# Cross attention in pairs of units: scores four units ahead, output projection and next keys between transpositions and scores

## The chip, the cores and the metric

One core of one Trainium2 chip. The time is that of one execution on the device, in microseconds (us); three runs of the kernel before gave a median of 2062.98.

## What is computed

A decoder layer with post-layer-norm on x (64 sequences of 128 tokens, width 128) with a context of 120 tokens a sequence, all float32:

```
x = LN(x + linear_attention(x))        # 16 heads of width 8, cumulative sums
x = LN(x + cross_attention(ctx, x))    # 16 heads of width 64
x = LN(x + experts(x))                 # 8 experts, 2 a token, and a shared MLP
```

Cross attention, where the change is, takes x as the queries and the normalised context together with the normalised x (120 + 128 = 248 rows) as keys and values:

```
q = lat @ Wq; k, v = split(concat(LN(ctx), lat) @ Wkv)
attn = softmax(q k^T * 64**-0.5); out = (attn @ v) @ Wout
```

## The kernel before

Three stages run one behind the other, each a block with one queue of instructions per engine: linear attention, cross attention and the experts. Each engine runs its queue in the order written in the Python loops; semaphores join them. There is no planner, the order is that of the code.

`cross_attention` (line 861) works through 32 rounds `r` of two sequences. A round has 8 pairs `j` of heads; with two sequences that is 16 units `s` (unit = one sequence, one pair of heads). The stages of one unit, with the engine that has each:

- `make_G` (TensorE, line 1304): for a pair of heads, queries times the product of Wq and Wk, as a three-part float32 product (`split_product`, line 853) into the one bank `ps_G`. `G_hi` (ScalarE, line 1106) rounds it into `G_part[0]`, `G_lo` (VectorE, line 1164) subtracts to get the rest into `G_part[1]`; only then is `ps_G` free. `G_part` has two buffers.
- `scores` (TensorE, line 1315): G times the keys for two heads, 6 matmuls of 248 columns, into one of three banks of `ps_S`.
- `maxima` (VectorE, line 1178) takes minus the maximum, `exponentials` (ScalarE, line 1110) the exponentials with their sums, `inverse` (VectorE, line 1183) the reciprocal, and `weights` (GpSimd, line 1033) the product, all in one of four rings of `prob`.
- four transpositions (TensorE, line 1368) into `ps_T` (two banks), and ScalarE's copy to `probT` (line 1128).
- `weighted_values` (TensorE, line 1331), once for each gang of four units, into the one bank `ps_O`; `out_copy` (VectorE, line 1174) moves it to `outT`.

Beside this, once a round: `output` (line 1322), the projection with `wo` of the round before, into `ps_V`, and `residual` (VectorE, line 1188), which adds it to X and takes the moments; `keys` (TensorE line 1267, VectorE line 1145), which turns the next round's rows into `ps_V`; eight `make_V` (line 1311), values into the same one bank `ps_V`, each copied by `V_copy` (VectorE, line 1170). Four small jobs of the routing for the experts are spread over the round: `turn_rows`, `logits` and `ranks` on TensorE (lines 307 to 329, all in `ps_O`), `turned_rows` and `scores_of` on ScalarE, and 26 small steps on VectorE (`route`, line 331) placed by the tables `ROUTE` and `ROUTE_LATE` (line 1230). GpSimd also splits the keys into two parts (`keys_hi`, `keys_lo`), normalises rows and issues four scatters a round; SyncE loads the context and the latents of later rounds.

TensorE's `body` (line 1352) does for each unit `s`: the transpositions of unit s, then `scores` of unit s + 3 (`LEAD`). Even units follow with `make_G` of the pair three ahead, odd ones with `make_V`. The output projection stands behind `make_G` of unit 2, the next keys behind `make_G` of unit 4, and a gang's weighted values at the end of every fourth unit (0, 4, 8, 12). The turn of the rows stands ahead of unit 10's transpositions and the logits ahead of unit 11's.

VectorE's `body` (line 1201) does for each unit: the copy of V (even units), next keys (unit 5), `G_lo` (odd units), `out_copy` (units 1, 5, 9, 13), residual (unit 3), the routing steps, then `maxima` of unit s + 3 and `inverse` of unit s + 2. ScalarE's (line 1117) does exponentials of unit s + 2, the copy of the transposed unit s, and on even units `G_hi`.

The last round computes scores, G, V and keys of a round 32 that isn't used, with the inputs of the first sequences loaded again (lines 970 to 973).

Of the kernel before, what the change touches and what calls it, by code (L numbers as in the profile page):

```python
# [27 lines left out]
S = 128  # L28
# [832 lines left out]
def cross_attention(nc, X, lat, ctx, ident, tri, later, slots):  # L861
# [19 lines left out]
    LEAD = 3  # L881
# [3 lines left out]
    MADE = FIRST[1] // 2 + 2  # L885
    U32 = mybir.dt.uint32
    with ExitStack() as stack:
# [61 lines left out]
        def _(sp):  # L949
# [34 lines left out]
            for par in range(2):  # L984
                sp.wait_ge(ctx_loaded[par], (ROUNDS // 2 + 1) * 16)
                sp.wait_ge(lat_loaded[par], (ROUNDS // 2 + 1) * 32)

        @block.gpsimd
        def _(pool):
# [49 lines left out]
            def body(r, par):  # L1039
                unit = r * UNITS  # L1040
                for s in range(UNITS):
                    weights(unit + s + 2, (s + 2) % RINGS)
# [8 lines left out]
                    if s == 6:  # L1051
                        keys_hi(r + 1, 1 - par)
                    if s == 7:
                        keys_lo(r + 1, 1 - par)
# [6 lines left out]
                    if s == 11:  # L1061
                        context_deviation(r + 2)
                    if s in (12, 13):
                        normalise_context(r + 2, par, s - 12)
# [29 lines left out]
        def _(act):  # L1094
# [22 lines left out]
            def body(r, par):  # L1117
                unit = r * UNITS
                for s in range(UNITS):
                    exponentials(unit + s + 2, (s + 2) % RINGS)  # L1120
                    if s == 10 and r:
# [3 lines left out]
                    if s == 12 and r:  # L1125
                        slots.scores_of(act, r - 1)
                    act.wait_ge(T_psum, unit + s + 1)
                    nc.scalar.copy(probT[0:KT, s % (2 * GANG)], ps_T[0:KT, s % 2, :]).then_inc(probT_ready, 1)  # L1128
                    if s % 2 == 0:
                        ahead = s // 2 + 3  # L1130
                        G_hi(r * PAIRS + ahead, ahead % 2)
# [5 lines left out]
            for k in range(2):  # L1137
                exponentials(k, k)
# [3 lines left out]
        def _(dve):  # L1142
# [58 lines left out]
            def body(r, par):  # L1201
                unit = r * UNITS
                for s in range(UNITS):
                    j = s // 2
                    if s == 0 and later_round(r):
                        V_copy(r * 8 + 3, 0, 1, 1)
                    if s and s % 2 == 0:
                        k = j - 1
                        V_copy(r * 8 + 4 + k, 1 - k // 4, k % 4 // 2, k % 2)
                    if s == 5:  # L1210
                        keys(r + 1)
                    if s % 2:
                        G_lo(r * PAIRS + j + 3, (j + 3) % 2)
                    if s % GANG == 1 and (s > 1 or later_round(r)):
                        out_copy(r * GANGS + s // GANG - 1, (s // GANG - 1) % GANGS)
                    if s == 3 and later_round(r):
                        residual(r - 1)
                    if r and s in ROUTE:
                        slots.route(dve, ps_O, r - 1, *ROUTE[s])
                    if r > 1 and s in ROUTE_LATE:  # L1220
                        slots.route(dve, ps_O, r - 2, *ROUTE_LATE[s])
                    if r == MADE:
                        for k in (s,) if s < 13 else (s * 2 - 13, s * 2 - 12):
                            slots.table(dve, 0, k)
                    maxima(unit + s + LEAD, (s + LEAD) % RINGS)
                    inverse(unit + s + 2, (s + 2) % RINGS)
                    if s == 7:
                        context_moments(r + 2, par)

# [29 lines left out]
            for k in range(2):  # L1259
# [6 lines left out]
        def _(pe):  # L1266
# [85 lines left out]
            def body(r, par):  # L1352
                unit = r * UNITS
                for s in range(UNITS):
                    j, u = s // 2, s % 2

                    if s == 10 and r:
                        pe.wait_ge(outT_ready, r * GANGS + 2)
                        slots.turn_rows(pe, ps_O, ident, r - 1)
                    if s == 11 and r:  # L1360
                        slots.logits(pe, ps_O, r - 1)
                    pe.wait_ge(prob_ready, unit + s + 1)
                    if unit + s > 1:
                        pe.wait_ge(probT_ready, unit + s - 1)
                    for h in range(2):
                        for tile in range(2):
                            at = (h * 2 + tile) * S
                            last = nc.tensor.transpose(ps_T[0:KT, s % 2, at:at + S], prob[:, s % RINGS, h, tile * KT:(tile + 1) * KT],  # L1368
                                                       ident[:])
                    last.then_inc(T_psum, 1)  # L1370

                    ahead = (s + LEAD) // 2
                    if u:
                        pe.wait_ge(G_lo_ready, r * PAIRS + ahead + 1)
                    scores((unit + s + LEAD) % BANKS, (s + LEAD) % 2, par if ahead < PAIRS else 1 - par, ahead % 2)

                    if u == 0:
                        ahead = j + 3
                        pe.wait_ge(G_lo_ready, r * PAIRS + ahead)
                        if s == 10:  # L1380
                            pe.wait_ge(kT_lo_ready, r + 2)
                        make_G(ahead % 2, par if ahead < PAIRS else 1 - par, ahead % PAIRS)
                    if s == 2 and later_round(r):
                        pe.wait_ge(V_ready, r * 8 + 5)
                        output(r - 1)
                    if s == 4:
                        pe.wait_ge(V_ready, r * 8 + 4 + 2)
                        keys(r + 1, 1 - par)
                    if u:
# [553 lines left out]
```

## Time and profile before

| | us |
|---|---|
| median of 3 runs | 2062.98 (2062.4 to 2067.14) |
| the profiled execution's own time | 2065.15 |
| its span, first to last instruction | 2063.4 |
| TensorE busy | 1966.8 |
| VectorE busy | 1508.9 |
| ScalarE busy | 1278.5 |
| GpSimd busy | 1307.8 |

The stages lie at about 0 to 266 us (linear attention), 266 to 1672 (cross attention) and 1672 to 2063 (experts). TensorE's end of a matmul is modelled and lies behind the next matmul's start, so the time that a matmul takes in a queue is read from start to start. Granted clock 1.00 is 2.4 GHz, 0.50 is 1.2 GHz.

### The profile page before, as it was taken

Reading aid. Unit: us, or ns where it says so; the run is one execution under the profiler, and the core shown is the slowest. Engines: PE = TensorE matmul, PEld = TensorE weight load, DVE = VectorE, ACT = ScalarE, POOL = GpSimd, SP = SyncE. Lnnn points to the kernel's source line nnn. Section 1 sums busy time; section 2 is a strip of 40 time slices with the busy share of each in tenths; the row PEclk is TensorE's granted clock in tenths of the full one; section 3 lists DMA queues with packets and bytes.
Section 4 is the critical chain, followed back from the end, with each engine's and each line's share of the span. In section 5 each row is a group of like instructions: output and inputs, shape, how many; then the busy total and the mean of one; then the engine's idle time right before and its main releaser. Section 6 shows DMA issues by size and latency. Waiting matters only on the chain. (4 is left out here: it accounts for less than half of the span.)

```text
span 2063.4 us, 47458 instructions
## 1 busy us (share of the span) xinstructions
PE 1966.8 (95%) x16023; PEld 1704.1 (83%) x16023; DVE 1508.9 (73%) x3953; ACT 1278.5 (62%) x3908; POOL 1307.8 (63%) x1462
## 2 busy tenths in 40 slices
PE   7999879999999999999999999999999989999976
PEld 4555469999999999999999999998899878788855
DVE  5999946777777777777777777778777755455575
ACT  4777646666666666666666666666666644444455
POOL 5888746666666666666666666666666664344476
PEclk9999979999999999999999999999999989999987
DMA  4200000000000000000000000001000022222354
GB/s 133 73 18 19 18 26 1 17 17 16 16 14 22 17 16 16 17 19 17 15 16 20 16 17 17 14 21 31 20 16 16 14 62 71 84 70 70 95 158 134
DMA packets 105023, 75.78 MB, mean 37 GB/s; under 512 B 11045, under 2 KB 98677, under 8 KB 104661
## 3 DMA queue, kind: packets, MB, share of 16 engines
q1 hardware_dynamic: 93732, 53.66, 9.3%
q0 software_dynamic: 8640, 17.97, 2.6%
q8 instruction: 135, 2.21, 0.4%
q10 hardware_dynamic: 2416, 1.12, 0.2%
q14 instruction: 100, 0.81, 0.1%
HBM read 40.15 MB, written 32.57 MB: 35 GB/s over the span
## 5 line engine op out<-in xcount | busy, mean ns | idle before, releaser
L1036 POOL TENSOR_TENSOR x_prob<-x_prob,x_inv 128x496 f32<-128x496 f32 x514 | 521.6, 1015 | 460.4 <-DVE x_inv L1186 457.7
L1114 ACT ACTIVATE x_prob<-x_ps_S,x_nmax 128x248 f32<-128x248 f32 x1028 | 472.7, 467 | 226.1 <-DVE x_nmax L1180 224.4
L1180 DVE TENSOR_REDUCE x_nmax<-x_ps_S 128x2 f32<-128x496 f32 x515 | 344.8, 670 | 105.0 <-PE x_ps_S L858 97.0
L1128 ACT COPY x_probT<-x_ps_T 124x512 f32<-124x512 f32 x512 | 300.2, 586 | 166.4 <-PE x_ps_T L1368 163.8
L856 PE MATMUL x_ps_S<-x_kT_lo,x_G_hi 128*128 128x248 f32 x1030 | 328.6, 319 | 0.0
L1368 PE MATMUL x_ps_T<-ident,x_prob 128*124 128x128 f32 x2048 | 319.0, 278 | 7.7 <-POOL x_prob L1036 6.4
L1368 PEld LDWEIGHTS x_ps_T<-ident,x_prob 128*124 128x124 f32 x2048 | 233.2, 140 | 73.9 <-POOL x_prob L1036 29.9
L858 PE MATMUL x_ps_S<-x_kT_hi,x_G_hi 128*128 128x248 f32 x1030 | 285.9, 278 | 0.0
L857 PE MATMUL x_ps_S<-x_kT_hi,x_G_lo 128*128 128x248 f32 x1030 | 285.7, 277 | 0.0
L1606 POOL DMA_INDIRECT sorted_results<-e_y,w_wkv x142 | 148.8, 1048 | 169.6 <-DVE e_y L1730 160.7
L1338 PE MATMUL x_ps_O<-x_probT,x_V 124*64 124x128 f32 x4096 | 251.9, 276 | 0.4 <-ACT x_probT L1128 0.4
L1166 DVE TENSOR_TENSOR x_G_lo<-x_ps_G,x_G_hi 128x512 fp32r<-128x512 f32 x259 | 177.9, 687 | 89.5 <-ACT x_G_hi L1108 89.2
L1338 PEld LDWEIGHTS x_ps_O<-x_probT,x_V 124*64 124x64 f32 x4096 | 221.0, 137 | 18.9 <-issue 5.2
L1114 ACT ACTIVATION_READ_ACCUMULATOR x_prob<-x_ps_S,x_nmax 128x1 f32 x1028 | 206.8, 201 | 0.0
L1108 ACT CAST x_G_hi<-x_ps_G 128x512 fp32r<-128x512 f32 x259 | 152.4, 589 | 75.3 <-PE x_ps_G L858 74.7
L857 PEld LDWEIGHTS x_ps_S<-x_kT_hi,x_G_lo 128*128 128x128 f32 x1030 | 195.7, 190 | 0.0
L856 PEld LDWEIGHTS x_ps_S<-x_kT_lo,x_G_hi 128*128 128x128 f32 x1030 | 194.8, 189 | 0.0
L858 PEld LDWEIGHTS x_ps_S<-x_kT_hi,x_G_hi 128*128 128x128 f32 x1030 | 194.2, 189 | 0.0
L1172 DVE COPY x_V<-x_ps_V 124x512 f32<-124x512 f32 x259 | 175.5, 678 | 2.6 <-PE x_ps_V L858 2.6
L628 POOL TENSOR_TENSOR lin_kv<-lin_qk,lin_v 128x1024 f32<-128x1024 f32 x64 | 135.4, 2137 | 23.1 <-DVE lin_qk L740 20.2
L281 POOL DMA_INDIRECT sorted_rows<-w_rows,slots_slot x128 | 132.3, 1034 | 28.0 <-issue 23.1
L856 PE MATMUL x_ps_G<-x_kT_lo,x_M_hi 128*128 128x256 f32 x518 | 146.2, 282 | 0.1
(246 smaller groups left out, 4474.7 us busy)
## 6 DMA issues: line engine op xcount, KB each, us to landing
w_wkv<-sorted_rows SPq DMA_DIRECT2D x142, 66.0 KB
e_back<-sorted_results SPq DMA_DIRECT2D x28, 256.0 KB, 3.6
x_nk<-latents SPq DMA_DIRECT2D x34, 124.0 KB
latents<-lin_nlat SPq DMA_DIRECT2D x32, 128.0 KB, 1.8
turned_rows<-w_rows SPq DMA_DIRECT2D x32, 128.0 KB, 1.7
w_wq<-turned_rows SPq DMA_DIRECT2D x32, 128.0 KB, 2.3
out_dram<-e_result SPq DMA_DIRECT2D x16, 256.0 KB, 3.6
x_nk<-in_ctx SPq DMA_DIRECT2D x34, 120.0 KB, 2.3
```

Of the source, the lines that this page charges most:

```text
L856: nc.tensor.matmul(out, stationary[0], moving[1], start=first, stop=False)
L857: nc.tensor.matmul(out, stationary[1], moving[0], start=False, stop=False)
L858: return nc.tensor.matmul(out, stationary[0], moving[0], start=False, stop=last)
L1036: nc.gpsimd.tensor_tensor(prob[:, k], prob[:, k], inv[:, k].unsqueeze(2).broadcast_to([P, 2, K]), ALU.mult).then_inc(prob_ready, 1)
L1108: nc.scalar.copy(G_part[0][:, pair], ps_G[:]).then_inc(G_hi_ready, 1)
L1114: nc.scalar.activation(prob[:, k, h, :], ps_S[:, n % BANKS, h * K:(h + 1) * K], ACT.Exp, bias=nmax[:, k, h:h + 1], accum_out=total[:, k, h ...
L1128: nc.scalar.copy(probT[0:KT, s % (2 * GANG)], ps_T[0:KT, s % 2, :]).then_inc(probT_ready, 1)
L1166: nc.vector.tensor_tensor(G_part[1][:, pair].rearrange("p h u q -> p (h u q)"), ps_G[:], G_part[0][:, pair].bitcast(F32).rearrange("p h u ...
L1172: nc.vector.tensor_copy(V[:, hf, u, tile, :], ps_V[0:KT, :]).then_inc(V_ready, 1)
L1180: nc.vector.tensor_reduce(nmax[:, k, :], ps_S[:, n % BANKS, 0:2 * K].rearrange("p (h k) -> p h k", h=2), AX, ALU.max, negate=True).then_in ...
L1338: last = nc.tensor.matmul(ps_O[h * DH:(h + 1) * DH, k * S:(k + 1) * S], V[:, j // 4, u, tile, (j % 4 * 2 + h) * DH:(j % 4 * 2 + h + 1) * D ...
L1368: last = nc.tensor.transpose(ps_T[0:KT, s % 2, at:at + S], prob[:, s % RINGS, h, tile * KT:(tile + 1) * KT], ident[:])
```

## The change

The loops of all four engines go by pairs. On TensorE a pair is: both units' transpositions, both units' scores (of the pair two ahead, `LEAD` = 4), `make_G` of the pair three ahead, the gang's weighted values on even pairs, `make_V`. The next keys (pair 2) and the output projection (pair 1) stand between the transpositions and the scores, the turn of the rows ahead of pair 5's transpositions, the logits behind pair 5's `make_G`, the ranks behind pair 1's. The second scores of a pair wait for the exponentials of a unit three before (`exp_ready`), since four units are under way with three banks.

On ScalarE: the two copies of transposed units, the exponentials of the first unit four ahead, `G_hi`, the exponentials of the second. On VectorE: V copy, inverse of the second unit of the pair before, routing, next keys or residual, two maxima, `out_copy` on even pairs, `G_lo`, inverse, routing. The queue of GpSimd keeps its order.

In the last round everything that belonged to a round 32 is left out, and so are the two loads at the end of SyncE's queue. Ahead of the rounds a fourth unit's scores, maximum and exponentials are done.

```diff
-    LEAD = 3
+    LEAD = 4
...
@@ sync
             for par in range(2):
-                sp.wait_ge(kT_psum, ROUNDS - 1 + par)
-                load(par * 2, par)
                 slots.store_turned(sp, ROUNDS - 3 + par)
...
@@ scalar
             def body(r, par):
                 unit = r * UNITS
+                for j in range(PAIRS):
+                    if j == 5 and r:
...
+                    for s in (2 * j, 2 * j + 1):
+                        act.wait_ge(T_psum, unit + s + 1)
+                        nc.scalar.copy(probT[0:KT, s % (2 * GANG)], ps_T[0:KT, s % 2, :]).then_inc(probT_ready, 1)
+                    if j == 6 and r:
                         slots.scores_of(act, r - 1)
+                    if unit + 2 * j + LEAD < ALL:
+                        exponentials(unit + 2 * j + LEAD, 2 * j % RINGS)
+                    if r < FINAL or j + 3 < PAIRS:
+                        G_hi(r * PAIRS + j + 3, (j + 3) % 2)
+                    if unit + 2 * j + LEAD < ALL:
+                        exponentials(unit + 2 * j + 1 + LEAD, (2 * j + 1) % RINGS)
...
@@ vector
             def body(r, par):
                 unit = r * UNITS
+                for j in range(PAIRS):
+                    s = 2 * j
+                    if j == 0 and r:
                         V_copy(r * 8 + 3, 0, 1, 1)
+                    if j and (r < FINAL or j < 5):
                         k = j - 1
                         V_copy(r * 8 + 4 + k, 1 - k // 4, k % 4 // 2, k % 2)
+                    if unit + s + 3 < ALL:
+                        inverse(unit + s + 3, (s + 3) % RINGS)
+                    routing(r, s)
+                    if j == 2 and r < FINAL:
                         keys(r + 1)
+                    if j == 1 and r:
+                        residual(r - 1)
+                    if unit + s + LEAD < ALL:
+                        maxima(unit + s + LEAD, s % RINGS)
+                        maxima(unit + s + 1 + LEAD, (s + 1) % RINGS)
+                    if j % 2 == 0 and (j or r):
+                        out_copy(r * GANGS + j // 2 - 1, (j // 2 - 1) % GANGS)
+                    if r < FINAL or j + 3 < PAIRS:
                         G_lo(r * PAIRS + j + 3, (j + 3) % 2)
+                    if unit + s + LEAD < ALL:
+                        inverse(unit + s + LEAD, s % RINGS)
+                    if j == 3 and r + 1 < FINAL:
                         context_moments(r + 2, par)
+                    routing(r, s + 1)
...
             maxima(2, 2)
-            for k in range(2):
+            maxima(3, 3)
+            for k in range(3):
                 inverse(k, k)
...
@@ tensor
             def body(r, par):
                 unit = r * UNITS
+                for j in range(PAIRS):
+                    first = unit + 2 * j
+                    if j == 5 and r:
                         pe.wait_ge(outT_ready, r * GANGS + 2)
                         slots.turn_rows(pe, ps_O, ident, r - 1)
+                    for s in (2 * j, 2 * j + 1):
+                        pe.wait_ge(prob_ready, unit + s + 1)
...
+                        last.then_inc(T_psum, 1)
+                    if j == 2 and r < FINAL:
+                        pe.wait_ge(V_ready, r * 8 + 4 + 2)
+                        keys(r + 1, 1 - par)
+                    if j == 1 and r:
+                        pe.wait_ge(V_ready, r * 8 + 5)
+                        output(r - 1)
+                    ahead = j + 2
+                    if r < FINAL or ahead < PAIRS:
                         pe.wait_ge(G_lo_ready, r * PAIRS + ahead + 1)
+                        for s in (2 * j, 2 * j + 1):
+                            if s % 2:
+                                pe.wait_ge(exp_ready, (first + 3) * 2)
+                            scores((unit + s + LEAD) % BANKS, s % 2, par if ahead < PAIRS else 1 - par, ahead % 2)
+
+                    ahead = j + 3
+                    if r < FINAL or ahead < PAIRS:
+                        if j == 5:
                             pe.wait_ge(kT_lo_ready, r + 2)
                         make_G(ahead % 2, par if ahead < PAIRS else 1 - par, ahead % PAIRS)
+                    if j == 5 and r:
+                        slots.logits(pe, ps_O, r - 1)
+                    if j % 2 == 0 and first:
...
+                        gang_output(r * GANGS + j // 2 - 1)
+                    if j == 1 and r > 1:
+                        pe.wait_ge(outT_ready, r * GANGS)
+                        slots.ranks(pe, ps_O, r - 2)
+                    if r < FINAL or j < 4:
...
                             pe.wait_ge(V_ready, r * 8 + 4 + j)
...
                         make_V(par if j < 4 else 1 - par, 1 - j // 4, j % 4 // 2, j % 2)
...
             scores(2, 0, 0, 1)
+            pe.wait_ge(exp_ready, 2)
+            scores(0, 1, 0, 1)
             rounds(pe, body)
```

## Rows read from the trace of the kernel before

**Rows 1.** The page: busy us of each engine, share of the span, instructions.

```profile
PE 1966.8 (95%) x16023; PEld 1704.1 (83%) x16023; DVE 1508.9 (73%) x3953; ACT 1278.5 (62%) x3908; POOL 1307.8 (63%) x1462
```

**Rows 2.** Windows: from:to, length, each engine's busy us, then PE clock, DMA share, GB/s.

```profile
420.00:1600.00 1180.00, 1175.32 (x11107) 1081.72 (x11104) 904.37 (x2462) 782.68 (x2475) 768.19 (x907) 1.00 0.06 18
1900.00:1985.00 85.00, 77.28 (x497) 65.25 (x497) 50.95 (x165) 41.26 (x128) 45.52 (x43) 0.97 0.36 105
```

**Rows 3.** The list of waits, 420 to 1600 us: total us, times, longest.

```profile
POOL x_prob L1036 <- DVE x_inv L1186: 387.3, 300, 4.7
```

**Rows 4.** Timeline of PE, one steady round: start us, us, engine, line, operation.

```profile
938.14 3.73 PE L1327 MATMUL x_ps_V<-w_wo,x_outT 128*128 128x128 f32 x32
...
943.02 0.40 PE L856 MATMUL x_ps_V<-x_wv_lo,x_kT_hi 128*124 128x512 f32 x1
...
943.73 0.60 PE L1368 MATMUL x_ps_T<-ident,x_prob 128*124 128x128 f32 x4
944.08 0.36 PE L856 MATMUL x_ps_S<-x_kT_lo,x_G_hi 128*128 128x248 f32 x1
...
944.85 0.28 PE L856 MATMUL x_ps_G<-x_kT_lo,x_M_hi 128*128 128x256 f32 x1
...
945.57 0.59 PE L1273 MATMUL x_ps_V<-ident,x_nk 124*128 124x124 f32 x4
946.09 1.97 PE L1338 MATMUL x_ps_O<-x_probT,x_V 124*64 124x128 f32 x32
947.99 0.65 PE L1368 MATMUL x_ps_T<-ident,x_prob 128*124 128x128 f32 x4
...
958.54 0.40 PE L856 MATMUL x_ps_V<-x_wv_lo,x_kT_hi 128*124 128x512 f32 x1
...
959.43 0.41 PE L311 MATMUL x_ps_O<-ident,w_rows 128*128 128x128 f32 x2
...
980.91 0.27 PE L1327 MATMUL x_ps_V<-w_wo,x_outT 128*128 128x128 f32 x1
```

**Rows 5.** Timeline of ACT, steady stretch.

```profile
907.29 0.47 ACT L1114 ACTIVATE x_prob<-x_ps_S,x_nmax 128x248 f32<-128x248 f32 x1 [0.82 <-DVE x_nmax L1180]
...
908.20 0.58 ACT L1128 COPY x_probT<-x_ps_T 124x512 f32<-124x512 f32 x1
909.13 0.59 ACT L1108 CAST x_G_hi<-x_ps_G 128x512 fp32r<-128x512 f32 x1 [0.35 <-PE x_ps_G L858]
```

**Rows 6.** Timeline of DVE, the same round as Rows 4.

```profile
941.91 0.42 DVE L1192 TENSOR_TENSOR slots_hsum<-x_ps_V,X 128x256 f32<-128x256 f32 x1 [2.26 <-PE x_ps_V L1327]
...
943.06 0.17 DVE L389 TENSOR_TENSOR slots_place<-x_ps_O,slots_base 128x16 f32<-128x16 f32 x1
...
948.10 0.69 DVE L1176 COPY x_outT<-x_ps_O 128x512 f32<-128x512 f32 x1 [0.33 <-PE x_ps_O L1338]
...
950.66 0.59 DVE L394 TENSOR_TENSOR slots_taken<-slots_chosen,slots_place 128x32 f32<-128x32 f32 x1
...
951.58 0.67 DVE L1180 TENSOR_REDUCE x_nmax<-x_ps_S 128x2 f32<-128x496 f32 x1
...
952.51 0.69 DVE L1166 TENSOR_TENSOR x_G_lo<-x_ps_G,x_G_hi 128x512 fp32r<-128x512 f32 x1 [0.19 <-ACT x_G_hi L1108]
...
968.28 0.16 DVE L365 TENSOR_REDUCE slots_col<-slots_score 128x2 f32<-128x16 f32 x1
...
968.98 0.67 DVE L1180 TENSOR_REDUCE x_nmax<-x_ps_S 128x2 f32<-128x496 f32 x1
...
970.24 0.16 DVE L373 TENSOR_REDUCE slots_col<-slots_order 128x2 f32<-128x16 f32 x1
...
971.41 0.67 DVE L1180 TENSOR_REDUCE x_nmax<-x_ps_S 128x2 f32<-128x496 f32 x1
```

**Rows 7.** Timeline, the end of cross attention.

```profile
1665.14 0.69 DVE L1176 COPY x_outT<-x_ps_O 128x512 f32<-128x512 f32 x1 [0.71 <-PE x_ps_O L1338]
...
1665.98 3.81 PE L1327 MATMUL x_ps_V<-w_wo,x_outT 128*128 128x128 f32 x32 [0.89 <-DVE x_outT L1176]
```

More of the change, by code:

```diff
@@ L885, in cross_attention @@
     MADE = FIRST[1] // 2 + 2
+    FINAL = ROUNDS - 1
     U32 = mybir.dt.uint32
@@ L1041, in body @@
                 for s in range(UNITS):
-                    weights(unit + s + 2, (s + 2) % RINGS)
+                    if unit + s + 2 < ROUNDS * UNITS:
+                        weights(unit + s + 2, (s + 2) % RINGS)
                     if s in (1, 3) and r > 2:
@@ L1118, in body @@
                 unit = r * UNITS
-                for s in range(UNITS):
-                    exponentials(unit + s + 2, (s + 2) % RINGS)
-                    if s == 10 and r:
+                for j in range(PAIRS):
+                    if j == 5 and r:
                         if r == 1:
@@ L1136, in _ @@
                 G_hi(j, j % 2)
-            for k in range(2):
+            for k in range(4):
                 exponentials(k, k)
@@ new lines, in body, with routing @@
+                    if j % 2 == 0 and (j or r):
+                        out_copy(r * GANGS + j // 2 - 1, (j // 2 - 1) % GANGS)
+                    if r < FINAL or j + 3 < PAIRS:
+                        G_lo(r * PAIRS + j + 3, (j + 3) % 2)
+                    if unit + s + LEAD < ALL:
+                        inverse(unit + s + LEAD, s % RINGS)
+                    if j == 3 and r + 1 < FINAL:
+                        context_moments(r + 2, par)
+                    routing(r, s + 1)
+            def routing(r, s):
+                if r and s in ROUTE:
+                    slots.route(dve, ps_O, r - 1, *ROUTE[s])
+                if r > 1 and s in ROUTE_LATE:
+                    slots.route(dve, ps_O, r - 2, *ROUTE_LATE[s])
+                if r == MADE:
+                    for k in (s,) if s < 13 else (s * 2 - 13, s * 2 - 12):
+                        slots.table(dve, 0, k)
@@ new lines, in body @@
+                    for s in (2 * j, 2 * j + 1):
+                        pe.wait_ge(prob_ready, unit + s + 1)
+                        if unit + s > 1:
+                            pe.wait_ge(probT_ready, unit + s - 1)
+                        for h in range(2):
+                            for tile in range(2):
+                                at = (h * 2 + tile) * S
+                                last = nc.tensor.transpose(ps_T[0:KT, s % 2, at:at + S],
+                                                           prob[:, s % RINGS, h, tile * KT:(tile + 1) * KT], ident[:])
+                        last.then_inc(T_psum, 1)
```

89 lines of the change are left out of this document (15 added, 74 removed).

## The prediction

> **What bounds the kernel now.** I read the page first, for the shares: TensorE (PE) is busy nearly all the span [rows 1]. Then the windows by stage: in the middle of cross attention PE is busy 1175 of 1180 us at full clock, while VectorE (DVE) has 904 and ScalarE (ACT) 783 [rows 2]. The list of waits shows where the slack is: POOL spends 387 us of the stage waiting for inverses [rows 3], and DVE idles 2.26 us ahead of each round's residual, waiting for the output projection [rows 6]. PE's timeline of one round gives its length, output to output, 42.77 us (938.14 to 980.91), and the price of each group of matmuls [rows 4]. So the stage is PE's queue, end to end, 32 times. A reordering can only take out PE's small holes, or open new ones by asking for something sooner than DVE, ACT or POOL can give it.
>
> The holes are small. The values product V takes 0.71 (943.02 to 943.73), but 0.89 before the turn of the rows (958.54 to 959.43): 0.2 of waiting. The same happens once more at the round's end, so about 0.4 us a round [rows 4].
>
> **Prices on PE.** Per unit 4 transpositions to the next group 0.35, scores 0.77, the queries' product G 0.72, next keys 0.52 with the change-over behind them, a gang of weighted values (call it O) 1.90, output 3.57 (3.73 less the 0.16 below) [rows 4]. Two units of transpositions in a row: three spacings of the four make 0.60 less 0.27, so 0.11 each; TT = 0.44 + 0.35 = 0.79. The first scores record behind transpositions is 0.36 long where others are 0.28, so SS = 0.77 + 0.69 = 1.46. Together 2.25, and two separate units make 2 x 1.12 = 2.24. **Pairing itself is worth nothing.** A pair is then TT, SS, G, V = 3.67, and with O (even pairs) 5.7.
>
> O is now followed by V and not by transpositions. Four transpositions behind O last 0.65 where others last 0.60 (947.99 against 943.73): 0.05 lost. I take 0.06 for V, bounds 0 and 0.2 (the keys' change-over is 0.1). The Trainium skill (TensorE: Matmul & The Clock Gate, "Step-by-step: what each phase is for") says that PE's queue pulls weight loads ahead of running matmuls; by that the change-over would be 0 and the sum some 7 us less (4 x 0.06 x 31), but the row shows that some of it stays.
>
> **Prices on the other engines.** DVE: maximum 0.67, rest G_lo 0.69, output copy 0.69 which starts 0.11 behind O's end, V copy 0.69 as its equal in size, each freeing DVE about 0.1 before it ends; residual and moments 1.15 (941.91 to 943.06); routing steps 0.92 for the three of pair 3 (950.66 to 951.58), 0.70 for the four at the end of pair 6, 1.17 for the five of pair 7 [rows 6]. ACT: a unit's exponentials 0.91 (907.29 to 908.20), G_hi 0.59 [rows 5]. Hand-overs: PE to the others 0.2 behind the group's end (six scores records in 0.77 are 0.12 apart and 0.28 long, so the modelled end lies 0.16 past the group's, and the residual starts 0.04 behind the output's modelled end: 938.14 + 3.73 against 941.91), DVE to PE 0.15 (1665.14 + 0.69 to 1665.98) [rows 7], ACT to DVE 0.03.
>
> **What the change tightens.** (a) Scores for pair j+2 need G_lo of the G made in pair j-1. Before, three units and more lay between; now only V and TT, 1.5 us, where there is no O. The chain is G end + 0.2, G_hi 0.59, G_lo 0.69, 0.15 = 1.65 at best. G_hi also stands behind the first exponentials (0.91), which stand behind the first maximum, which stands behind whatever DVE has at the pair's head: V copy, routing, residual. (b) The output projection moves from behind G to behind TT, and still needs the V copy of the pair before (they share a PSUM bank). (c) The next keys likewise.
>
> **A round, pair by pair**, in us from PE's start of pair 1, with DVE's queue in its written order (starts are those of a steady round, where pair 0 of the next comes out as pair 0 of this one):
> - Pair 0's O ends at -0.76. DVE: output copy from -0.64, G_lo from -0.04, inverse, V copy 0.65 to 1.34. PE has TT done at 0.79, output can start at 1.49: **hole 0.70**. Output to 5.07, scores 6.46, G 7.17, the ranks' two small matmuls (0.2, an estimate from the 0.11 between two), V to 8.09.
> - Behind the output DVE has the residual 5.27 to 6.42, then the maximum to 7.09; ACT exponentials to 8.02, G_hi to 8.61; DVE G_lo to 9.33, two routing steps, V copy 9.65 to 10.34. The keys of pair 2 (due 8.88) wait for that copy till 10.49: **hole 1.61**. DVE's idle time during the 3.5 us of output no longer helps, since all of this is queued behind the residual.
> - Pair 2: scores to 12.38, O to 15.08, V to 15.84. Output copy and G_lo behind O end at 16.49, due 16.63: no hole.
> - Pair 3: DVE V copy to 17.18, three routing steps to 18.1, maximum 18.75, exponentials 19.68, G_hi 20.27, G_lo 20.99; pair 4's scores (due 20.30) start 21.14: **hole 0.84**.
> - Pair 5: the turn waits for the output copy as now: 0.20. Its G_lo (31.19) and pair 7's meet their due times with nothing left.
> - Pair 6: DVE after O: output copy, G_lo to 36.93, four routing steps to 37.62. Pair 7: V copy, five steps to 39.5, maximum 40.17, exponentials 41.1, G_hi 41.69, G_lo 42.41. Next pair 0's scores, due 40.74, start at 42.56: **hole 1.82**.
>
> Sum of holes 5.2. The round becomes 42.8 - 0.4 + 5.2 = 47.6, **+4.7**, or about 4.75 by the direct count. Thirty such intervals: +141.
>
> **What costs nothing.** A probability is due two pairs behind its scores. POOL's work is 1.74 us a unit, everything in it (768 us over 27.6 rounds of 16 units [rows 2]). Pair 3's first exponentials end at 19.68, the inverse comes behind G_lo at 21.1 and the transposition is due 26.5: covered. Tightest is the round's end, inverse at 38.3, transposition 40.2: 1.9 us for 1.74 of work. Cover gone, it would be another 1 us a round. The new wait of the second scores for the exponentials (three banks, lead four) falls due 2 us or more behind them (pair 1's at 8.02, asked for at 11.7). SP loses the two last loads and their waits; its store of turned rows and the row loads behind move up, and nobody waits for those in this trace. ACT's reordering adds no work.
>
> **Ends.** In the last round PE loses 3 units of scores (3 x 0.77), 3 G (2.2), 4 V (2.8) and the keys (0.5): 7.8, at the prices of [rows 4], of which 0.8 comes back as waits for the last probability copy: -7.0. The last round still has the holes of pairs 1 to 4, about +2. Start: the fourth scores and maximum stand ahead of the first inverse: +1. Round 0 has a few small holes of type (a): +1.
>
> **Sum.** 141 + 2 + 2 - 7 = +138 on the profiled execution's own 2065.15 (span 2063.4), which lies 0.1% above the median of 2062.98 and inside the runs shown. 2203; I say 2200. The measurement can tell about 0.3% (6 us) from no change.
>
> **Rivals.**
> 1. *The chain holds* (faster). If G_lo, V copy and output copy come in time after all, only holes go: 0.4 x 31 = -13 and -7 at the end: 2045. For it: DVE is only 77% busy, ACT 66% [rows 2]. Against: the 1.65 against 1.5 of (a) has no slack even with both engines idle. It decides where G_lo lands within 1.5 us of G. 6%; 4% for holes and gains that cancel (within 0.3%).
> 2. *Half the holes.* DVE's work is fixed, so what is late in one pair may be early in the next, and the residual's and routing's delays may be partly taken up. Only (b), the pair 0 hole and 0.3 on odd pairs: about 2 to 3 a round, 2105 to 2150. 16%.
> 3. *The clock falls too.* PE would be busy about 89% of the stage, with holes near 2 us twice a round. At 91% busy in the expert stage the granted clock was 0.97 [rows 2]. With 0.96 here, 8% of the time at 1.2 GHz, up to 4% more of 1330 us: +50, so 2250. 12%. The Trainium skill (TensorE: Matmul & The Clock Gate, "HAM oscillation — how this bites in real kernels") tells of waits between groups of matmuls that let the clock down; no row of the cross stage here shows it, as PE never pauses there.
> 4. My forecast, holes as listed with errors of a third: 2150 to 2240. 62%.
>
> The range takes 4, most of 2 and the edge of 3: 2120 to 2245. Faster 6%, same 4%, slower 90%.
>
> **What would show it.** Output-to-output near 47.5. PE idle ahead of the output (L1327's successor) and of the key transpositions, released by the V copy; ahead of scores in pairs 4 and 0, released by G_lo. In the list of waits, PE or PEld behind x_V and x_G_lo, some 100 us and more in total where there is nothing now; POOL's wait for the inverse larger. PE's busy time 8 to 10 us less. The expert stage as long as before. Wrong if the round stays under 44, or if the holes stand elsewhere, above all ahead of transpositions on POOL.

## The result and the profile after

The change makes the kernel slower: 2267.12 us (median of 4 runs, 2266.35 to 2269.51) against 2062.69 in the runs beside it, a ratio of 1.099 (95% interval 1.0968 to 1.1011). The forecast was 2200, with a range to 2245. The profiled executions differ by 201.4 us of span (2264.8 against 2063.4).

The page of the kernel after, the line that answers to [rows 1], and the stage's window that answers to the first of [rows 2]:

```profile
PE 2016.5 (89%) x15971; PEld 1731.6 (76%) x15971; DVE 1512.4 (67%) x3932; ACT 1251.3 (55%) x3897; POOL 1293.1 (57%) x1450
```

```profile
420.00:1600.00 1180.00, 1063.31 (x9612) 966.12 (x9611) 787.43 (x2123) 659.30 (x2137) 658.72 (x786) 0.98 0.05 15
```

TensorE, which had 4.7 us idle in this window, now has 117. VectorE, ScalarE and GpSimd do less in it too: nobody became the bound, all four wait for each other. So the time went into the order. The list of waits of the same window shows for whom:

```profile
POOL x_prob L1036 <- DVE x_inv L1190: 447.5, 190, 5.9
ACT x_prob L1115 <- DVE x_nmax L1184: 412.5, 190, 5.7
...
PE x_ps_S L856 <- DVE x_G_lo L1170: 79.8, 47, 2.8
...
PE x_ps_V L1288 <- DVE x_V L1176: 29.8, 24, 2.3
...
PE x_ps_V L1342 <- DVE x_V L1176: 7.0, 24, 0.4
```

The last three are the forecast's places with the forecast's releasers: scores (L856 into `ps_S`) wait for `G_lo`, keys (L1288) and output (L1342) for the V copy. 47 waits over 24 rounds are two a round. The list of before has none of them. The first answers to [rows 3].

TensorE's timeline gives the size of each hole. A pair's transpositions (8) take 0.79 from start to start where nothing waits, so what lies between their start and the next group's beyond 0.79 is the hole, the time that TensorE stands still there:

```profile
1076.30 1.18 PE L1381 MATMUL x_ps_T<-ident,x_prob 128*124 128x128 f32 x8
1080.30 0.38 PE L856 MATMUL x_ps_S<-x_kT_lo,x_G_hi 128*128 128x248 f32 x1 [2.83 <-DVE x_G_lo L1170]
...
1082.59 1.97 PE L1353 MATMUL x_ps_O<-x_probT,x_V 124*64 124x128 f32 x32
1084.49 0.49 PE L856 MATMUL x_ps_V<-x_wv_lo,x_kT_hi 128*124 128x512 f32 x1
...
1085.28 1.03 PE L1381 MATMUL x_ps_T<-ident,x_prob 128*124 128x128 f32 x8
1086.61 3.84 PE L1342 MATMUL x_ps_V<-w_wo,x_outT 128*128 128x128 f32 x32 [0.29 <-DVE x_V L1176]
1090.20 0.36 PE L856 MATMUL x_ps_S<-x_kT_lo,x_G_hi 128*128 128x248 f32 x1
...
1093.30 1.04 PE L1381 MATMUL x_ps_T<-ident,x_prob 128*124 128x128 f32 x8
1095.86 0.64 PE L1288 MATMUL x_ps_V<-ident,x_nk 124*128 124x124 f32 x4 [1.53 <-DVE x_V L1176]
```

Pair 0: 1080.30 - 1076.30 - 0.79 = 3.21. Output: 1.33 - 0.79 = 0.54. Keys: 1.77 in this round, 1.42 as the median of 22. The same reading at pair 4 gives 0.76, and the turn of rows 0.16. V behind O (1085.28 - 1084.49) takes 0.79 to 0.80 where it takes 0.70 elsewhere.

From output to output, a round was 42.8 us; now 15 of the 30 steady intervals are near 48.6, 12 near 50.15 and 3 longer (51.3, 51.4, 53.9); together 1489.3 against 1288.4, so **201 us of the 201.4 are in the rounds**. At the ends little is left over: the first output comes 5.1 later after the kernel's start, the last interval is 3.9 shorter (34.49 against 38.43), the way to the experts 1.0 longer, and the experts take 389.1 instead of 390.9.

Why 50.15? Windows (columns as in [rows 2]), two of the stretch behind one pair 0 hole, then one around the same hole a round later:

```profile
1029.50:1033.00 3.50, 2.90 (x18) 2.75 (x18) 3.33 (x11) 1.70 (x6) 1.40 (x2) 0.78 0.00 0
1033.00:1036.50 3.50, 3.50 (x36) 3.16 (x36) 1.22 (x3) 2.39 (x9) 1.63 (x2) 0.73 0.06 19
1076.00:1084.00 8.00, 5.17 (x54) 4.48 (x55) 6.65 (x18) 4.01 (x14) 3.81 (x5) 1.00 0.05 17
```

And the weighted values behind the first of these holes:

```profile
1033.07 2.84 PE L1353 MATMUL x_ps_O<-x_probT,x_V 124*64 124x128 f32 x32
```

They are 2.84 long, and 1.97 behind the second. Some matmuls of this stretch run at 1.2 GHz; it costs that round 1.55 us. Counted over the rounds: 30 x 48.6 = 1458, and 31 us lie above it, against 4 above 30 x 42.8 before. So the holes cost 30 x 5.8 = 174 us, and the 27 that are left go with the clock. They are a difference, and a few of them can be something else: two of the three longer rounds have a half-clock stretch twice as long (granted clock 0.93 over 788 to 840 and over 1334 to 1386 us), but the third, of 53.9, is the round that also makes the experts' table, which took 45.5 before.

### The profile page after: what moved, and what is told of

Read it like the earlier page. It is cut to its first block and busy times, and to the rows that moved or that the text cites. A ratio compares the mean times of both kernels' runs of the same rounds, so it can differ in the third digit from the quotient of the medians.

```text
span 2264.8 us, 47256 instructions
## 1 busy us (share of the span) xinstructions
PE 2016.5 (89%) x15971; PEld 1731.6 (76%) x15971; DVE 1512.4 (67%) x3932; ACT 1251.3 (55%) x3897; POOL 1293.1 (57%) x1450
## 3 DMA queue, kind: packets, MB, share of 16 engines
q10 hardware_dynamic: 2416, 1.12, 0.2%
## 5 line engine op out<-in xcount | busy, mean ns | idle before, releaser
L1036 POOL TENSOR_TENSOR x_prob<-x_prob,x_inv 128x496 f32<-128x496 f32 x512 | 516.7, 1012 | 672.6 <-DVE x_inv L1190 605.8
L856 PE MATMUL x_ps_S<-x_kT_lo,x_G_hi 128*128 128x248 f32 x1024 | 310.1, 303 | 102.9 <-DVE x_G_lo L1170 101.9
L1127 ACT COPY x_probT<-x_ps_T 124x512 f32<-124x512 f32 x512 | 277.6, 602 | 127.9 <-PE x_ps_T L1381 126.0
L1184 DVE TENSOR_REDUCE x_nmax<-x_ps_S 128x2 f32<-128x496 f32 x512 | 324.9, 664 | 31.8 <-PE x_ps_S L858 30.9
L856 PEld LDWEIGHTS x_ps_S<-x_kT_lo,x_G_hi 128*128 128x128 f32 x1024 | 196.4, 192 | 119.1 <-DVE x_G_lo L1170 117.8
L1381 PE MATMUL x_ps_T<-ident,x_prob 128*124 128x128 f32 x2048 | 270.4, 274 | 2.3 <-POOL x_prob L1036 2.2
L1353 PE MATMUL x_ps_O<-x_probT,x_V 124*64 124x128 f32 x4096 | 262.2, 283 | 1.1 <-ACT x_probT L1127 0.7
L1353 PEld LDWEIGHTS x_ps_O<-x_probT,x_V 124*64 124x64 f32 x4096 | 231.3, 142 | 20.0 <-issue 3.6
L1180 DVE COPY x_outT<-x_ps_O 128x512 f32<-128x512 f32 x128 | 88.5, 691 | 207.4 <-PE x_ps_O L1353 207.2
L1115 ACT ACTIVATION_READ_ACCUMULATOR x_prob<-x_ps_S,x_nmax 128x1 f32 x1024 | 212.9, 208 | 0.0
L857 PE MATMUL x_ps_G<-x_kT_hi,x_M_lo 128*128 128x256 f32 x512 | 148.9, 291 | 0.0
```

The source lines that it names most:

```text
L856: nc.tensor.matmul(out, stationary[0], moving[1], start=first, stop=False)
L857: nc.tensor.matmul(out, stationary[1], moving[0], start=False, stop=False)
L1036: nc.gpsimd.tensor_tensor(prob[:, k], prob[:, k], inv[:, k].unsqueeze(2).broadcast_to([P, 2, K]), ALU.mult).then_inc(prob_ready, 1)
L1115: nc.scalar.activation(prob[:, k, h, :], ps_S[:, n % BANKS, h * K:(h + 1) * K], ACT.Exp, bias=nmax[:, k, h:h + 1], accum_out=total[:, k, h ...
L1184: nc.vector.tensor_reduce(nmax[:, k, :], ps_S[:, n % BANKS, 0:2 * K].rearrange("p (h k) -> p h k", h=2), AX, ALU.max, negate=True).then_in ...
L1353: last = nc.tensor.matmul(ps_O[h * DH:(h + 1) * DH, k * S:(k + 1) * S], V[:, j // 4, u, tile, (j % 4 * 2 + h) * DH:(j % 4 * 2 + h + 1) * D ...
```

## Why the pair 0 hole is 3.2 us

The forecast had 1.82 there. VectorE's timeline, from the end of pair 6 through pair 7 to pair 0's wait:

```profile
1073.62 0.82 DVE L369 TENSOR_TENSOR slots_equal<-slots_score,slots_col 128x16 f32<-128x16 f32 x1
1074.48 0.17 DVE L371 SCALAR_TENSOR_TENSOR slots_order<-slots_equal,slots_index 128x16 f32<-128x16 f32 x1
1074.58 0.68 DVE L1176 COPY x_V<-x_ps_V 124x512 f32<-124x512 f32 x1
...
1075.43 1.38 DVE L375 TENSOR_TENSOR slots_chosen<-slots_order,slots_col 128x16 f32<-128x16 f32 x1
...
1077.35 1.25 DVE L1184 TENSOR_REDUCE x_nmax<-x_ps_S 128x2 f32<-128x496 f32 x2
1079.56 0.69 DVE L1170 TENSOR_TENSOR x_G_lo<-x_ps_G,x_G_hi 128x512 fp32r<-128x512 f32 x1 [0.96 <-ACT x_G_hi L1109]
```

Two steps of 16 elements take 0.82 and 1.38. In the trace before, which the forecast was priced from, they took 0.18 and 0.42. GpSimd in the same stretch:

```profile
1073.40 1.01 POOL L1036 TENSOR_TENSOR x_prob<-x_prob,x_inv 128x496 f32<-128x496 f32 x1 [2.23 <-DVE slots_col L365]
1074.59 1.12 POOL L281 DMA_INDIRECT sorted_rows<-w_rows,slots_slot  x1 [0.17 <-issue]
1075.74 1.02 POOL L1036 TENSOR_TENSOR x_prob<-x_prob,x_inv 128x496 f32<-128x496 f32 x1
```

The product ends at 74.41, the L369 step at 74.44; the next product at 76.76, the L375 step at 76.81. The small step with two SBUF inputs stands still while the product, which also reads SBUF, runs, and ends 0.03 to 0.05 us behind it. (The second step began at 75.43, ahead of that product but 0.28 before the end of GpSimd's issue of a scatter, and alone it would have been done before the product. An issue as such holds no step: the one of line 381, with two SBUF inputs too, lies wholly under the next issue and takes 0.17. What held the second step until the product began stays open.) The copy of V, which reads PSUM alone, and the maximum are not touched. The two lines over the whole kernel (least/median/most ns), before and then after:

```profile
L369 DVE TENSOR_TENSOR slots_equal<-slots_score,slots_col x32: 174/174/191, 369.3 to 1684.8; 128x16 f32<-128x16 f32 x32
L375 DVE TENSOR_TENSOR slots_chosen<-slots_order,slots_col x64: 174/176/429, 371.1 to 1687.3; 128x16 f32<-128x16 f32 x64
```

```profile
L369 DVE TENSOR_TENSOR slots_equal<-slots_score,slots_col x32: 175/824/827, 379.3 to 1888.0; 128x16 f32<-128x16 f32 x32
L375 DVE TENSOR_TENSOR slots_chosen<-slots_order,slots_col x64: 174/824/1503, 381.1 to 1890.5; 128x16 f32<-128x16 f32 x64
```

Before, the order of the queues kept the four steps of pair 6 wholly apart from the products, and the five of pair 7 met only the end of one. VectorE and GpSimd in the round that the forecast was read from:

```profile
970.43 0.42 DVE L375 TENSOR_TENSOR slots_chosen<-slots_order,slots_col 128x16 f32<-128x16 f32 x1
...
971.32 0.18 DVE L381 TENSOR_TENSOR slots_equal<-slots_rest,slots_col 128x16 f32<-128x16 f32 x1
```

```profile
969.81 1.01 POOL L1036 TENSOR_TENSOR x_prob<-x_prob,x_inv 128x496 f32<-128x496 f32 x1 [1.72 <-DVE x_inv L1186]
970.80 0.79 POOL L1012 TENSOR_SCALAR x_nk<-x_nk,x_cmom,x_crstd 120x128 f32<-120x128 f32 x1
```

The product ended at 70.82 and the L375 step at 70.85. So the standing still was there before the change, and the 0.59 of the L394 step in [rows 6] is another case of it. The change set the inverse, which starts a product, right ahead of the routing steps. Four steps at the end of pair 6 take 1.34 (forecast 0.70) and the five of pair 7 2.1 (1.17): 1.6 us more, on the chain that ends in pair 0's `G_lo`.

The Trainium skill (SBUF — State Buffer, "Who interferes with whom") says that a VectorE instruction with two SBUF inputs contends with a GpSimd instruction that reads SBUF, and that one with at most one SBUF input, outside the 2-port perf modes, doesn't. For the product the traces agree: the median of L369 is 174 ns without one beside it and 824 with one. They don't agree for every GpSimd instruction that reads SBUF: the L381 step above lies wholly under GpSimd's TENSOR_SCALAR of line 1012, which reads `x_nk` in SBUF, and takes 0.18 (174 to 176 ns in each of the 31 rounds in which it lies so).

## The experiments

The kernel before ran at 2060.71 beside the first four, and at 2063.68 beside the other four. Kernel 1 is that of experiment 1, and so on; an undisturbed round is one without half-clock stretches.

**1. Routing steps behind `G_lo`**, to get those that stood ahead of the maxima off the chain. The four at the end of pair 6 still stand ahead of pair 7's maxima.

```diff
-                    routing(r, s)
                     if j == 2 and r < FINAL:
                         keys(r + 1)
...
+                    routing(r, s)
                     routing(r, s + 1)
```

> The changed kernel, with VectorE's routing steps of a pair all behind G_lo and its inverse, none ahead of the maxima. Theory A (order of VectorE's queue: what stands ahead of the first maximum delays G_lo, and G_lo the scores two pairs later): the hole ahead of pair 0's scores shrinks from 3.2 us by the 2.0 us of the five steps to about 1.2, the one ahead of pair 4's (0.76) goes, the other two stay, 0.5 ahead of the output and 1.4 to 1.8 ahead of the keys. A round 48.6 to about 45.9, and if the half-clock stretches go with the 3.2 us hole, no 50.1 rounds: 2267 to about 2165. Theory B (the holes come from the shorter distance between G and scores alone, wherever VectorE does its routing): the late maxima move by less than 0.5 us and the time stays above 2240. Against A alone: the 11 steps now behind pair 7's G_lo could delay pair 0's copies, which would show as a longer hole ahead of the output.

2205.42, ratio 1.0700 (1.0669 to 1.0731). A round is 47.4, and its clock doesn't fall; 45.9 and about 2165 were expected. The pair 0 hole falls from 3.21 to 1.11 and that of pair 4 from 0.76 to 0.28, so the five routing steps of pair 7 were two thirds of the large hole. But eleven steps in a row now stand ahead of the V copies of pairs 0 and 1: the output's hole grows from 0.54 to 1.44, and pair 6 has a new one of 0.43. Waits of the stage, where the rows for L1342 and `x_ps_S` have changed places:

```profile
PE x_ps_V L1342 <- DVE x_V L1176: 31.4, 25, 2.3
...
PE x_ps_S L856 <- DVE x_G_lo L1170: 23.6, 51, 1.1
```

**2. `G_hi` ahead of both exponentials**, ScalarE's part of the chain.

```diff
-                    if unit + 2 * j + LEAD < ALL:
-                        exponentials(unit + 2 * j + LEAD, 2 * j % RINGS)
                     if r < FINAL or j + 3 < PAIRS:
                         G_hi(r * PAIRS + j + 3, (j + 3) % 2)
                     if unit + 2 * j + LEAD < ALL:
+                        exponentials(unit + 2 * j + LEAD, 2 * j % RINGS)
+                    if unit + 2 * j + LEAD < ALL:
                         exponentials(unit + 2 * j + 1 + LEAD, (2 * j + 1) % RINGS)
```

> The changed kernel, with ScalarE's G_hi ahead of the first exponentials of the pair. Theory A (G_hi waits behind the exponentials, these behind the first maximum): G_lo then follows the second maximum directly, where it now idles 0.96 us for G_hi, so the holes of pair 0 (3.2), pair 2's keys (1.4 to 1.8) and pair 4 (0.76) each shrink by 0.8 to 1.0: a round about 2.6 us less, 2267 to about 2185. Theory B (VectorE's lateness alone sets G_lo, ScalarE's order does not matter): within 10 us of 2267. Cost possible on this side: exponentials and so probabilities 0.6 us later, which had 1 us and more of room.

2206.29, ratio 1.0704 (1.0673 to 1.0735). The undisturbed round is 46.6: 2.0 less, where 2.6 were expected. But 23 of the 30 rounds are near 48.1, with a half-clock stretch (stage clock 0.97), and the time is 2206 instead of the 2185 expected. Pair 0 fell to 2.16 and pair 4 to 0.07, as worked out; the keys only from 1.42 to 1.12, because their V copy also waits behind the residual. What is left of the pair 0 hole is VectorE's own queue.

**3. Output projection behind `make_G`**, where the kernel before has it, with the residual behind `G_lo`.

```diff
-                    if j == 1 and r:
-                        residual(r - 1)
                     if unit + s + LEAD < ALL:
                         maxima(unit + s + LEAD, s % RINGS)
...
                         inverse(unit + s + LEAD, s % RINGS)
+                    if j == 1 and r:
+                        residual(r - 1)
...
-                    if j == 1 and r:
-                        pe.wait_ge(V_ready, r * 8 + 5)
-                        output(r - 1)
                     ahead = j + 2
...
                         make_G(ahead % 2, par if ahead < PAIRS else 1 - par, ahead % PAIRS)
+                    if j == 1 and r:
+                        pe.wait_ge(V_ready, r * 8 + 5)
+                        output(r - 1)
```

> The changed kernel, with the output projection back behind pair 1's G and the residual behind its G_lo on VectorE; all else as changed. Theory A (output in front of the scores puts the residual's 1.2 us and the maxima behind it in one chain ahead of the next keys): the 0.5 us hole ahead of the output goes, that ahead of the keys shrinks from 1.4 to 1.8 to about 0.3, a new one of about 0.75 opens ahead of V, which waits for the residual's first sum: a round 1.1 to 1.3 us less, 2267 to about 2230. Theory B (the keys' hole comes from the keys' own place): no change beyond the 0.5, or none. The pair 0 hole of 3.2 stays in both.

2252.48, ratio 1.0928 (1.0897 to 1.0960). The undisturbed round is 47.37, 1.23 less: the output's hole is 0 and that of the keys 0.16, while V now waits 0.62 for the residual's sum. That is as expected, but the time is 2252 instead of 2230: fewer rounds stay undisturbed, and the time falls by less than half of 30 x 1.23. The stage's window says why: granted clock 0.95, the lowest of all eight kernels.

```profile
420.00:1600.00 1180.00, 1089.56 (x9674) 996.68 (x9673) 800.22 (x2141) 668.26 (x2150) 663.86 (x788) 0.95 0.05 14
```

**4. GpSimd's product at half its size.** The probabilities of each unit's second head stay unnormalised; nothing else changes. This measures the standing still by itself.

```diff
-                nc.gpsimd.tensor_tensor(prob[:, k], prob[:, k], inv[:, k].unsqueeze(2).broadcast_to([P, 2, K]), ALU.mult
+                nc.gpsimd.tensor_tensor(prob[:, k, 0:1], prob[:, k, 0:1], inv[:, k, 0:1].unsqueeze(2).broadcast_to([P, 1, K]), ALU.mult
```

> The changed kernel, with GpSimd's product of probabilities and inverses done for the first head of each unit only (the second head's probabilities stay unnormalised): 0.5 us in place of 1.0, nothing else touched. Theory C (routing steps with two inputs in SBUF stand still while GpSimd's product runs and end 0.03 us behind it; that is why those of pair 6 and 7 take 0.82 and 1.4 where they took 0.17 and 0.42 before): their durations fall by up to 0.5 us each, the pair 0 hole from 3.2 to 2.3 to 2.7, a round 0.5 to 0.9 less. Theory D (the steps are long for another reason, the semaphore between them or the table's other work): durations and the hole unchanged, time within 5 us of 2267.

2212.2, ratio 1.0733 (1.0684 to 1.0782), an undisturbed round of 47.37: 1.23 less, where 0.5 to 0.9 were expected. That is 37 of the 55 us; the rest goes with fewer half-clock stretches (stage clock 0.99). No instruction of VectorE was edited, yet its steps became shorter with GpSimd's:

```profile
L369 DVE TENSOR_TENSOR slots_equal<-slots_score,slots_col x32: 174/408/412, 375.9 to 1830.4; 128x16 f32<-128x16 f32 x32
L375 DVE TENSOR_TENSOR slots_chosen<-slots_order,slots_col x64: 174/408/967, 377.3 to 1832.9; 128x16 f32<-128x16 f32 x64
```

824 became 408 and 1.38 became 0.97, together 0.82 us, and the pair 0 hole is 2.39 instead of 3.21, 0.82 less. The step of line 394 in pair 3 went from 0.57 to 0.17, and the hole ahead of pair 4's scores from 0.76 to 0.35; that second part had been overlooked when the round was estimated. No rival that was named explains this: the duration of a 16-element step follows the length of another engine's instruction, and the holes follow the steps.

**5. Next keys behind `make_G`**, with VectorE's part behind the maxima.

```diff
-                    if j == 2 and r < FINAL:
-                        keys(r + 1)
...
                         maxima(unit + s + 1 + LEAD, (s + 1) % RINGS)
+                    if j == 2 and r < FINAL:
+                        keys(r + 1)
...
-                    if j == 2 and r < FINAL:
-                        pe.wait_ge(V_ready, r * 8 + 4 + 2)
-                        keys(r + 1, 1 - par)
...
+                    if j == 2 and r < FINAL:
+                        pe.wait_ge(V_ready, r * 8 + 4 + 2)
+                        keys(r + 1, 1 - par)
                     if j % 2 == 0 and first:
```

> The changed kernel, with the next keys back behind pair 2's G (VectorE's part behind the maxima); the output projection stays in front of the scores. Theory A (the keys wait for a copy of V that comes 1.4 us late at their place, and would find it done 2.2 us further on): the 1.42 us hole goes and no other grows, a round 1.3 to 1.5 us less, 2267 to about 2222. Theory E (the lateness only moves on: G_lo of pair 1 then holds up pair 2's scores): the same time shows ahead of those scores as 0.2 to 0.5, and the gain is 1.0 us a round or less.

2216.86, ratio 1.0745 (1.0725 to 1.0765). A round is 47.72, only 0.88 less than 48.6: the 1.42 ahead of the keys is gone, but 0.48 appears ahead of the same pair's scores, which wait for `G_lo` (74 waits of TensorE for it instead of 47, three a round instead of two). VectorE is still late by that much in this pair, and only the place where it shows has moved. The time falls by 50 us, twice what 30 x 0.88 makes, for the stage's clock is 1.00 here, with the pair 0 hole at 3.22 as before.

```profile
420.00:1600.00 1180.00, 1080.81 (x9912) 980.35 (x9911) 821.73 (x2202) 680.92 (x2205) 683.18 (x809) 1.00 0.05 16
```

**6. The edits of 1, 2, 3 and 5 together**, with the pairs, the lead of four and the last round as the change has them.

> The changed kernel with the four edits together: routing behind G_lo, G_hi ahead of the first exponentials, output and keys behind G. Theory A: the holes left are about 0.3 to 1.0 ahead of pair 0's scores (3.2 less 2.0 less 1.0, and what G_hi, G_lo and the hand-overs take beyond V and the transpositions), 0.62 for the residual's sum, 0.1 to 0.4 ahead of pairs 2, 4 and 6: a round 44.0 to 44.8, no half-clock rounds, 2105 to 2125, still above the kernel before by 2 to 3%, since G and the scores that need it stay one pair apart. If the pairs themselves, and not what stands in the queues, cost the time, it stays above 2160.

2110.09, ratio 1.0227 (1.0209 to 1.0246), a round of 44.46, clock 1.00. So 157 of the 204 us, those of the clock among them, lie in where four steps stand in their queues. What remains a round is V's wait for the residual's sum, and scores of pairs 4, 0 and 1 waiting for `G_lo` (0.08, 0.14 and 0.83). The stage's two largest waits of TensorE:

```profile
PE x_ps_S L856 <- DVE x_G_lo L1170: 15.8, 27, 0.6
...
PE x_ps_V L856 <- DVE slots_hsum L1196: 10.6, 27, 0.4
```

**7. The kernel before with the short last round**, the one part of the change that the forecast priced as a gain. Guards of this kind in all bodies:

```diff
-                    weights(unit + s + 2, (s + 2) % RINGS)
+                    if unit + s + 2 < ALL:
+                        weights(unit + s + 2, (s + 2) % RINGS)
...
-            pe.wait_ge(V_ready, ROUNDS * 8 + 3)
+            pe.wait_ge(V_ready, ROUNDS * 8)
```

> The kernel before, with only the last round's unused work (scores, G, V, keys of a round 32, and the two loads) left out as in the change. The prediction's term: 7.8 us of TensorE's work less, 0.8 back: 7 us faster, 0.9966. If the end is set by the chain of the last probabilities and the residual instead, under 3 us.

2060.76, ratio 0.9985 (0.9976 to 0.9994): 3 us where 7 were forecast. The last interval is 35.57 instead of 38.43. By the forecast's prices TensorE does 7.8 us less, but with nothing to do between, it waits at the last hand-overs:

```profile
1648.67 0.61 PE L318 MATMUL x_ps_O<-slots_gwT,w_rows 128*128 128x8 f32 x4 [0.73 <-ACT w_rows L299]
...
1656.16 0.66 PE L1372 MATMUL x_ps_T<-ident,x_prob 128*124 128x128 f32 x4 [1.64 <-POOL x_prob L1036]
...
1657.49 3.63 PE L1342 MATMUL x_ps_O<-x_probT,x_V 124*64 124x128 f32 x32 [0.67 <-ACT x_probT L1130]
```

These waits make 3.04 us, where the same stretch had 0.39 before: the first two were covered by the unused work. And the last weighted values are 3.63 long, where they took 1.97 before: the granted clock is 0.72 over 1656 to 1662 us, against 1.00 there before. So 2.65 us of what was missing are waits and 1.7 are half clock, in the profiled execution. In kernel 8, which has the same end, the last weighted values take 1.97 and the last interval is 34.31.

**8. Kernel 7 with the two 0.2 us holes of [rows 4] closed**, by moving routing steps from the slots ahead of the output copies to later ones.

```diff
-            ROUTE = {11: (0, 2), 13: (2, 6), 14: (6, 11), 15: (11, 17)}
-            ROUTE_LATE = {3: (RANK_STEP, SLOT_STEP), 6: (SLOT_STEP, 22), 8: (22, STEPS)}
+            ROUTE = {11: (0, 2), 13: (2, 6), 14: (6, 10), 15: (10, 14)}
+            ROUTE_LATE = {0: (14, 17), 3: (RANK_STEP, SLOT_STEP), 6: (SLOT_STEP, 22), 10: (22, STEPS)}
...
             rounds(dve, body)
+            slots.route(dve, ps_O, ROUNDS - 2, 14, 17)
```

> The kernel of the run before this one, with ten of VectorE's routing steps placed elsewhere: those from 22 on at unit 10 in place of 8, and 14 to 16 at unit 0 of the next round. If the two holes of 0.2 us a round on TensorE come from these steps (the first of them takes 1.16 us where GpSimd's product runs, ahead of the output copy that the turn waits for), both go: 0.3 to 0.4 us a round, 10 to 13 us faster than that run. If the probabilities' chain sets them, within 3 us of it.

2048.61, ratio 0.9928 (0.9915 to 0.9942): faster than both kernels, and 12 us less than kernel 7, where 10 to 13 were expected. A round is 42.37, and the turn of the rows starts with no wait ahead of it:

```profile
1019.79 3.73 PE L1332 MATMUL x_ps_V<-w_wo,x_outT 128*128 128x128 f32 x32
...
1040.89 0.38 PE L311 MATMUL x_ps_O<-ident,w_rows 128*128 128x128 f32 x2
...
1062.17 3.73 PE L1332 MATMUL x_ps_V<-w_wo,x_outT 128*128 128x128 f32 x32
```

So the forecast's reading of those 0.2 us holes was right, and they can be closed without regrouping the units.

## Why the prediction was right in kind and too low

| step of the forecast | forecast, us | measured |
|---|---|---|
| output waits for V copy, a round | 0.70 | 0.54 |
| keys wait for V copy | 1.61 | 1.42 |
| pair 4 scores wait for `G_lo` | 0.84 | 0.76 |
| turn of rows | 0.20 | 0.16 |
| pair 0 scores wait for `G_lo` | 1.82 | **3.21** |
| change-over from O to V, each of four | 0.06 | 0.10 |
| a round | +4.7 | +5.8 |
| clock | 0 | **+27 in all** |
| thirty rounds | +141 | +201 |
| start of the stage | +2 | +5 |
| last round | -5 | -3 to -4 |
| experts | 0 | -2 |

**Right:** the main case. Every hole is where it was put, with the releaser that was named, and pairing itself brought nothing: a pair without a hole takes TensorE 3.66 us, as two separate units did. Four of the five holes were forecast 0.04 to 0.19 above what they are. The experts are as long as before within 2 us.

**The step that failed** is "routing steps ... 0.70 for the four at the end of pair 6, 1.17 for the five of pair 7". These prices were read from a round in which no GpSimd product ran beside the four and only the end of one beside the five, and were taken over into a queue that starts one right ahead of them. What they measured is 1.34 and 2.1. Kernels 1 and 4 show it from two sides. It makes 1.4 us a round, some 42 us of the 63 that were missing; the four smaller holes give back 0.5 us a round and the change-overs take 0.16.

**Mis-sized too:** the clock had been set apart as a rival ("Rival 3", 0.96 and +50 at most) at 12%. It came together with the main case instead of in its place, at half that price: 0.98, +27 us. Two cases that can hold at once have to be added, which would have put the forecast's own upper end above 2245. And with it fell "PE's busy time 8 to 10 us less": it is 50 more (2016.5 against 1966.8). Matmuls at half clock are longer, but that is the smaller part: kernel 1, whose stage clock is 1.00, still has 2003.0, and kernel 7, with as many matmuls and next to no holes, 1953.8. At each hole the modelled tail of the last group counts, which lay under the next group before (eight transpositions are 1.18 long in their record ahead of the hole, and 0.79 from start to start where none follows). The Trainium skill's tale of waits between groups that let the clock down (TensorE: Matmul & The Clock Gate, "HAM oscillation — how this bites in real kernels") holds here for kernels 3 and 2 and the change, at 0.95, 0.97 and 0.98; kernels 5 and 1, with waits in every round too, stay at 1.00.

**The ends:** -7 for the work left out in the last round took the unused work as fully on the path, with 0.8 us of waits in its place. Kernel 7 shows -3: 2.65 us of waits came in its place, and in the profiled execution a half-clock stretch of 1.7 us.

**Slips of arithmetic** changed little: with the forecast's own 1.46 for both units' scores, those of pair 1 end at 6.53 and not at 6.46, which makes the keys' hole 1.54; and 2 to 3 us a round, in rival 2, add up to about 2120 to 2150, not 2105.

**The change-over** of 0.10 is the upper of the two rows that the forecast had (the keys' 0.1), not the nearer-looking one. The rule of the Trainium skill cited there (TensorE: Matmul & The Clock Gate, "Step-by-step: what each phase is for"), weight loads pulled ahead of running matmuls, was taken to make it 0; behind the weighted values this trace shows 0.10.

**Left open:** what decides whether the clock falls behind a hole. The change and kernels 3 and 5 have the same 3.2 us hole each round, with stage clocks of 0.98, 0.95 and 1.00, and in the change it falls in about every second round. In kernel 2 the largest hole is 2.16 and the stage clock 0.97. The size of the largest hole alone doesn't set it. No run was made that varies one hole by itself.

## What to carry to other kernels

- Grouping units shortens the distance between a producer's chain and its consumer. Where TensorE is the bound and its queue is full, count for each consumer the chain over the other engines (here 1.65 us at best) against the work left between (1.5): if it doesn't fit on paper, every delay on those queues comes on top of it. Small side jobs belong behind the chain's link, not ahead of it.
- A small instruction's duration is a price only for the neighbours it had. Look at what the other engine does at the moment, and at least/median/most of the line: 174/176/429 was a warning in the trace before, and so was the 0.59 in [rows 6] for a step of 32 elements.
- Work whose result isn't used may still cover waits; here, leaving out 7.8 us of it was worth 3.

## What the runs showed of the hardware

- A VectorE step of 16 elements with two SBUF inputs lasts 0.17 us alone, 0.82 under a 1.0 us GpSimd product that began 0.22 us before it, 1.38 in the median and at most 1.50 where it begins in the last 0.3 us of the issue of a scatter that a product follows, and 0.41 when the product is halved. Under the rest of such an issue, and under GpSimd's TENSOR_SCALAR of 128 elements that reads SBUF, it takes 0.17 to 0.20. Steps that read one SBUF input, or one in PSUM and one in SBUF, keep their 0.16 to 0.17.
- The same hole of 3.2 us a round went with a stage clock of 1.00, 0.98 or 0.95, depending on what else stood in the round.
- V behind 32 matmuls of the weighted values takes 0.10 us longer than behind G (0.80 against 0.70).
